# Narrower query chunks and evenly spaced tiles in an attention and FFN kernel

## The chip, the cores and the metric

The program runs on one core of one Trainium2 chip. The metric is the time of one execution on the device in microseconds (us). Before the change it is 531.16 us, the median of 3 runs (530.85 to 532.54). PE is TensorE, PEld its weight loads, DVE VectorE, ACT ScalarE, POOL GpSimd, SP SyncE.

## The reference

One layer over x of 2048 rows and 128 features: an attention with 16 heads of 8 features that has a silu in place of a softmax, then an FFN of width 352 with weights and activations rounded to FP4 in blocks of 16. All values are float32.

```python
x_proj = jax.nn.silu(x @ W1 + b1)
u, v, q, k = jnp.split(x_proj, 4, axis=-1)
scores = jnp.einsum('bqhd,bkhd->bhqk', qh, kh)
attn = jax.nn.silu(scores) / S
av = jnp.einsum('bhqk,bkhd->bqhd', attn, vh).reshape(B, S, D)
y = _layernorm(av * u, gamma, beta) @ W2 + b2
x = _layernorm(x + y)
h = jax.nn.silu(fp4_linear(x, w_gate)) * fp4_linear(x, w_up)
x = _layernorm(x + fp4_linear(h, w_down))
```

## The kernel before

Each of the 16 heads has a silu over 2048 x 2048 scores. The work is cut into chunks of queries (`WIDTHS`), and a chunk of width w into steps: a step takes one tile of 128 keys, and as many heads as fill four banks of 512 columns, twice (`a` = 0, 1). A chunk of 256 queries has 32 steps, two groups of 16 key tiles; one of 128 queries has 16. There are 256 steps, whatever the widths. `BEGIN` holds the first step of each chunk; before, 0, 32, 64, 96, 128, 160, 192, 208, 224, 240.

In a step `at`, PE writes the scores of the step (`scores`, ps<-q_stack,k_stack), in three pairs of PSUM banks that go round (`SB`), then the sums attn x v of the step two earlier (`times_v`, ps<-attn,v_pad; `LAG` = 2), then at most one other job (`job`). ACT applies the silu to each half of the scores (attn<-ps, 128x1024), two a step, and holds three steps of them (`RING`). The scores use bfloat16 parts stacked so that one matmul of 64 rows gives float32 accuracy; the sums are float32 matmuls of 32 columns that the records show in two passes.

The sums of a chunk gather in bank 6 or 7, by turns (`AV`). Meanwhile the other of the two is the spare bank for jobs. When a chunk is done, DVE takes its sums out, times u, into the buffer `zu` (`take_av`, called at the job step LAG after the next chunk's begin). Everything behind the attention is done in 16 tiles of 128 rows. A tile has six jobs on PE, in the spare bank: y (transpose of zu and product with W2), xqT, gate, up, hqT, down. DVE empties the bank after each (two adds or copies, and for y an add only after the row statistics, whose inverse root POOL computes), except gate, which ACT empties with a silu. Between y and xqT, and between up and hqT, DVE does the FP4 rounding in some nine operations; after down it does the last layer norm, and SP writes the tile out. The jobs' steps are a table written by hand (`TILE_AT`: a base step and an offset for each piece); tile 15 comes after all steps.

The engines run their own lists in order and wait on semaphores. Three waits of PE matter. A job waits until the job before it has been emptied, and until `take_av` has been done for the chunk before the one whose sums are being made (`av_taken`). The first sums of a chunk wait until the last job that used their bank has been emptied (`wait_spare`). Scores wait until ACT has read the bank. DVE's list holds the work of each job at the job's step, all of it up to the next job's, so `take_av` stands behind the whole chain of an earlier job.

Of the kernel before, what the change touches and what calls it, by code (L numbers as in the profile page):

```python
# [12 lines left out]
P = 128  # L13
# [9 lines left out]
K_TERMS = (0, 1, 0, 1, 2, 0)  # L23


WIDTHS = (256,) * 6 + (128,) * 4


class Count:
# [10 lines left out]
def build(nc, x, W1, b1, W2, b2, gamma, beta, w_gate, w_up, w_down, out):  # L40
    _, S, D = x.shape
    FF = w_gate.shape[0]
    HD = 8
    CH = 512
    NCH = S // CH
    KT = S // P
    TPC = CH // P
    SLOTS = 8
    M = 4
    FEAT = 3  # L50
    PARTS = 5
    TERMS = len(Q_TERMS)
    RING = 3
    SB = 3
    LAG = 2
# [4 lines left out]
    NBD = D // BLOCK  # L60
    assert D == P and len(FT) == 3 and sum(WIDTHS) == S

# [3 lines left out]

    Q0 = [sum(WIDTHS[:c]) for c in range(len(WIDTHS))]
    STEPS = [(c, g, i) for c, w in enumerate(WIDTHS) for g in range(M * w // CH) for i in range(KT)]
    BEGIN = [STEPS.index((c, 0, 0)) for c in range(len(WIDTHS))] + [len(STEPS)]

    M_ORDER = (0, 2, 1, 3)

    def ms(c, g):

        per = CH // WIDTHS[c]
        return M_ORDER[g * per:(g + 1) * per]

    AV = [6 + c % 2 for c in range(len(WIDTHS))]

# [7 lines left out]
               24: ("q", 1536), 27: ("w2", 0), 29: ("gate", 0), 31: ("up", 0), 33: ("down", 0)}  # L87

    TAIL = KT - 1
    WIDE, DENSE = KT - 6, KT - 2  # L90
    EVEN = {"y": 3, "xqT": 7, "gate": 9, "up": 11, "hqT": 15, "down": 17}
    ODD = {"y": 18, "xqT": 22, "gate": 24, "up": 26, "hqT": 30, "down": 31}
    TILE_AT = {t: (BEGIN[t // 2 + 1], ODD if t % 2 else EVEN) for t in range(WIDE)}
    for t in range(WIDE, DENSE):
        TILE_AT[t] = (BEGIN[WIDE // 2 + 1] + LAG + 12 * (t - WIDE),
                      {"y": 0, "xqT": 4, "gate": 5, "up": 7, "hqT": 10, "down": 11})
    TILE_AT[DENSE] = (BEGIN[-2] + LAG, {"y": 0, "xqT": 4, "gate": 6, "up": 8, "hqT": 12, "down": 13})
    JOB_AT = {at: (kind, i, None) for at, (kind, i) in PREP_AT.items()}
    for t, (base, offsets) in TILE_AT.items():
        JOB_AT |= {base + d: (kind, 0, t) for kind, d in offsets.items()}  # L100
    JOBS = [JOB_AT[at] for at in sorted(JOB_AT)]
    JOB_BANK = [spare_bank(at) for at in sorted(JOB_AT)]
    job_no = {job: k for k, job in enumerate(JOBS)}
    ACT_JOBS = [k for k, (kind, i, tile) in enumerate(JOBS)
                if kind in ("k", "q", "v", "u") or (kind == "gate" and tile is not None)]
    VEC_JOBS = [k for k in range(len(JOBS)) if k not in ACT_JOBS]

    def chunk_of(tile):
        return max(c for c in range(len(WIDTHS)) if Q0[c] <= tile * P)


    UNITS = [("k", 0, 256), ("q", 0, 256), ("k", 256, 512), ("k", 768, 512), ("k", 1280, 512), ("k", 1792, 256),
# [3 lines left out]
    with ExitStack() as ctx:  # L116
        def sb(name, shape, dt=F32):
            return ctx.enter_context(nc.sbuf_tensor(name, shape, dt))

        def sem(name):  # L120
            return ctx.enter_context(nc.semaphore(name))

        ps = ctx.enter_context(nc.psum_tensor("ps", [P, 8, CH], F32))
# [33 lines left out]
        xT = sb("xT", [D, S])  # L157
        feat = sb("feat", [P, FEAT, CH])
        parts = sb("parts", [P, PARTS, 3, CH], BF16)
        uT = sb("uT", [P, S])  # L160
# [4 lines left out]
        k_stack = sb("k_stack", [P, SLOTS, S], BF16)  # L165
        q_stack = sb("q_stack", [P, SLOTS, S], BF16)
        attn = sb("attn", [P, RING, 2, 2, CH])
        zu = sb("zu", [P, CH])

        class Rows:  # L170

# [10 lines left out]
        xqT = sb("xqT", [D, 2, P])  # L182
# [19 lines left out]
        job_made, job_by_act, job_by_vec = sem("job_made"), sem("job_by_act"), sem("job_by_vec")  # L202
# [31 lines left out]
        def stack(eng, n, chosen=range(TERMS), by_pool=False):  # L234
# [3 lines left out]
            for part in range(3):  # L238
                eng.wait_ge(split_done, 3 * n + part + 1)
                for t in (t for t in chosen if terms[t] == part):  # L240
                    eng.dma_start(to[t::8, :, start:start + w], parts[:, n % PARTS, part, 0:w]).then_inc(done, 16)

# [3 lines left out]
        def wait_stack(eng, n):  # L246
            if n < len(SHARES):
                eng.wait_ge(stacked[n], 16 * len(SHARES[n][0]))
                eng.wait_ge(stacked_by_pool[n], 16 * len(SHARES[n][1]))
            else:  # L250
                eng.wait_ge(stacked[n], 16 * TERMS)
# [128 lines left out]
        def _(pe):  # L380
            def mm(to, lhsT, rhs, start=True, stop=True):
                return pe.matmul(to, lhsT, rhs, start=start, stop=stop, skip_group_check=True)  # L382
# [139 lines left out]

            def y_of(tile, small, off):

                c = chunk_of(tile)
                z = zu[:, tile * P - Q0[c]:(tile + 1) * P - Q0[c]]
                pe.transpose(ps[:, small, off:off + P], z, ident[:, :])  # L527
                return mm(ps[:, small, off + P:off + 2 * P], z, w2_centred[:, :])

# [11 lines left out]
            def behind(kind, tile, bank):  # L541
                r = ROWS[tile % 2]
                if kind == "y":
                    return y_of(tile, bank, 0)
                if kind == "xqT":
                    pe.wait_ge(xq_ready, tile + 1)
                    return pe.transpose(ps[:, bank, 0:P], r.xn[:, 0:D], ident[:, :])
                if kind == "gate":
                    return mm(ps[:, bank, 0:FF], xqT[:, tile % 2, :], wgate_t[:, :])
                if kind == "up":  # L550
                    return mm(ps[:, bank, 0:FF], xqT[:, tile % 2, :], wup_t[:, :])
                if kind == "hqT":
                    pe.wait_ge(hq_ready, tile + 1)
                    return hqT_of(r, bank)
                return down_of(r, bank, 0)
# [16 lines left out]
            for i in range(KT - TAIL):  # L572
                y_of(TAIL + i, TAIL_SMALL[i], 0).then_inc(tail_y, 1)
# [20 lines left out]
        def _(act):  # L594
            def silu(to, frm, **kw):
                return act.activation(to, frm, ACT.Silu, **kw)  # L596
# [5 lines left out]
            def project(kind, c, bank):  # L602
# [7 lines left out]
                w = UNITS[n][2]  # L610
                if n >= FEAT:
                    act.wait_ge(split_done, 3 * (n - FEAT + 1))
                return silu(feat[:, n % FEAT, 0:w], ps[:, bank, 0:w],
                            bias=b1_col[:, 1:2] if kind == "q" else b1_col[:, 2:3])
# [60 lines left out]
        def _(dve):  # L675
# [16 lines left out]
            def split(kind, start):  # L692
# [4 lines left out]
                else:  # L697
                    dve.wait_ge(job_by_act, ACT_JOBS.index(job_no[(kind, start, None)]) + 1)
                if n >= PARTS:
                    wait_stack(dve, n - PARTS)  # L700
                f, p = feat[:, n % FEAT, 0:w], parts[:, n % PARTS, :, 0:w]
                dve.tensor_copy(p[:, 0, :], f).then_inc(split_done, 1)  # L702
# [51 lines left out]
            def take_av(c):  # L754

                w = WIDTHS[c]
                dve.wait_ge(av_done, BEGIN[c + 1])
                for tile in range(TAIL):
                    if chunk_of(tile) == c - 1:
                        dve.wait_ge(job_made, job_no[("y", 0, tile)] + 1)  # L760
                dve.scalar_tensor_tensor(out=zu[:, 0:w], in0=ps[:, AV[c], 0:w], scalar=1.0 / S,
                                         in1=uT[:, Q0[c]:Q0[c] + w], op0=ALU.mult, op1=ALU.mult).then_inc(av_taken, 1)

            def statistics(src, which, r):
# [129 lines left out]
            for at in range(BEGIN[1], len(STEPS)):  # L894
                if at - LAG in BEGIN:
                    take_av(BEGIN.index(at - LAG) - 1)
                kind, _, tile = JOB_AT.get(at, (None, None, None))
                if tile is None:
                    continue
                if kind == "y":  # L900
                    to_quantised_x(tile)
                elif kind == "xqT":
                    copy_xqT(tile)
                elif kind == "up":
                    to_quantised_h(tile)
                elif kind == "hqT":
                    copy_hqT(tile)
                elif kind == "down":
                    to_out(tile)

            take_av(len(WIDTHS) - 1)
            for i, r in enumerate(TAIL_ROWS):
                dve.wait_ge(tail_y, i + 1)
# [38 lines left out]
```

## Time and profile before

| | |
|---|---|
| median of 3 runs | 531.16 us |
| the profiled execution | 531.98 us, span 530.0 us |
| busy PE, ACT, DVE, POOL | 96%, 93%, 40%, 12% of the span |
| first and last step's activations | 16.84 us to 507.2 us |
| granted TensorE clock | 0.997 of full speed in the mean, 9 tenths or more in every slice but one |
| DMA busy | almost all before 80 us |

The page gives one execution. Busy time of PE is modelled from pipelined matmuls, so a busy PE may still be waiting; the views in order of time tell more. A line is often that of a helper (`mm`, `silu`), so groups are read by the names of what they write and read. ACT's activations overlap: one starts about 0.9 us after the one before, and lasts 1.02 us or more.

### The profile page before, as it was taken

The numbers are of one execution on the slowest core, as the hardware profiler recorded it, in microseconds if no ns is written. First come the engines' busy times: TensorE is split into PE (matmuls) and PEld (weight loads), VectorE is DVE, ScalarE is ACT, GpSimd is POOL, SyncE is SP. The second block draws the span as 40 slices with busy tenths as digits, with TensorE's granted clock in tenths as the row PEclk, the third lists the DMA queues.
The fourth block names the chain that finished last, engine by engine and source line by source line (L and its number), as shares of the span: only waits on it lengthen the run. The fifth ranks groups of instructions, "written<-read, shape, count | busy, mean of one in ns | idle before, by whom it ended". The sixth has DMA issues, their size and how long they took to land.

```text
span 530.0 us, 18169 instructions
## 1 busy us (share of the span) xinstructions
PE 510.5 (96%) x8116; PEld 268.8 (51%) x8116; DVE 210.2 (40%) x621; ACT 493.1 (93%) x558; POOL 63.4 (12%) x152
## 2 busy tenths in 40 slices
PE   7799999999999999999999999999999999999996
PEld 5354444444444444444444444444477777777753
DVE  4644642243433332333333332333343444544344
ACT  4799999999999999999999999999999999999920
POOL 6940000101010100101010100101010110101010
PEclk9899999999999999999999999999999999999999
DMA  4891240000000000000000000000000000000000
GB/s 125 219 189 29 66 119 2 2 2 7 1 7 2 6 2 8 1 2 6 2 8 1 7 1 7 1 2 8 1 9 2 9 9 3 9 4 7 4 6 7
DMA packets 13576, 12.00 MB, mean 23 GB/s; under 512 B 1589, under 2 KB 12858, under 8 KB 13498
## 3 DMA queue, kind: packets, MB, share of 16 engines
q1 hardware_dynamic: 12650, 9.05, 6.9%
q0 software_dynamic: 704, 1.66, 1.3%
q8 instruction: 64, 1.05, 0.8%
q10 hardware_dynamic: 144, 0.13, 0.1%
q14 instruction: 14, 0.11, 0.1%
HBM read 1.92 MB, written 1.05 MB: 6 GB/s over the span
## 4 chain that ended last, share of the span: by engine, by line
ACT 45%; PE 39%; issue 10%; DVE 3%; DMA 1%; POOL 1%; SPq 0%; POOLq 0%; DVEq 0%; ACTq 0%
ACT attn L596 44%; PE ps L382 36%; PE ps L532 1%; DMA k_stack<-parts 1%; PE ps L414 1%; POOL rstd_b L370 1%; PE ps L527 0%; DMA xn_b<-in_L_attn_b 0%; DVE parts L702 0%; DVE stats_b L765 0%; ACT gate_a L596 0%; POOL ve_b L369 0%; DVE mv_b L767 0%; DVE x_b L770 0%; ACT feat L596 0%
## 5 line engine op out<-in xcount | busy, mean ns | idle before, releaser
L596 ACT ACTIVATE attn<-ps 128x1024 f32<-128x1024 f32 x512 | 477.5, 1125 | 7.2 <-PE ps L382 5.7
L382 PE MATMUL ps<-attn,v_pad 128*32 128x256 f32 (+1 forms) x5120 | 275.4, 342 | 0.4 <-DVE wdown_t L890 0.3
L382 PE MATMUL ps<-q_stack,k_stack 64*128 64x256 bf16 (+1 forms) x2560 | 170.3, 251 | 8.2 <-DMA q_stack<-parts 1.4
L382 PEld LDWEIGHTS ps<-attn,v_pad 128*32 128x32 f32 x5120 | 132.5, 109 | 80.8 <-issue 37.9
L382 PEld LDWEIGHTS ps<-q_stack,k_stack 64*128 64x128 bf16 x2560 | 81.2, 94 | 119.6 <-ACT attn L596 75.8
L369 POOL TENSOR_TENSOR ve_a<-mv_a,eps_col 128x1 f32<-128x1 f32 x24 | 4.5, 189 | 270.1 <-DVE mv_a L767 270.1
L815 DVE TENSOR_TENSOR gate_a<-gate_a,ps 128x352 f32<-128x352 f32 x8 | 4.2, 521 | 58.7 <-PE ps L382 58.7
L369 POOL TENSOR_TENSOR ve_b<-mv_b,eps_col 128x1 f32<-128x1 f32 x24 | 4.6, 190 | 177.2 <-DVE mv_b L767 177.2
L815 DVE TENSOR_TENSOR gate_b<-gate_b,ps 128x352 f32<-128x352 f32 x7 | 3.6, 521 | 50.6 <-PE ps L382 50.6
L382 PE MATMUL ps<-zeros 128*128 128x512 bf16 x63 | 15.7, 399 | 1.2 <-DVE zeros L836 1.2
L702 DVE CAST parts<-feat 128x512 bf16<-128x512 f32 (+1 forms) x10 | 6.1, 611 | 25.6 <-ACT feat L596 25.6
L382 PE MATMUL ps<-wgate_t,xqT 128*128 128x352 f32 x32 | 13.7, 511 | 0.0
L382 PE MATMUL ps<-wup_t,xqT 128*128 128x352 f32 x32 | 13.6, 508 | 0.0
L370 POOL TENSOR_TENSOR rstd_a<-ve_a,minus_half 128x1 f32<-128x1 f32 x24 | 13.2, 550 | 1.9
L370 POOL TENSOR_TENSOR rstd_b<-ve_b,minus_half 128x1 f32<-128x1 f32 x24 | 13.2, 548 | 1.9
L770 DVE TENSOR_SCALAR x_b<-x1p_b,mv_b,rstd_b 128x128 f32<-128x128 f32 x16 | 5.5, 347 | 14.9 <-POOL rstd_b L370 14.9
L770 DVE TENSOR_SCALAR x_a<-x1p_a,mv_a,rstd_a 128x128 f32<-128x128 f32 x16 | 5.5, 347 | 14.9 <-POOL rstd_a L370 14.9
L829 DVE TENSOR_TENSOR x1p_a<-ps,x_a 128x128 f32<-128x128 f32 x8 | 2.3, 292 | 22.6 <-PE ps L382 22.6
L382 PE MATMUL ps<-xT,w_qk 128*128 128x512 f32 (+1 forms) x20 | 10.3, 612 | 0.5 <-ACT xT L627 0.5
L382 PEld LDWEIGHTS ps<-zeros 128*128 128x128 bf16 x63 | 6.2, 101 | 8.2 <-issue 1.2
L823 DVE COPY hqT_a<-ps 128x256 f32<-128x256 f32 x8 | 3.4, 425 | 16.7 <-PE ps L532 16.7
L765 DVE BATCH_NORM_STATS2 stats_a<-ps 128x6 f32<-128x128 f32 x8 | 2.4, 298 | 19.0 <-PE ps L382 19.0
(153 smaller groups left out, 345.0 us busy)
## 6 DMA issues: line engine op xcount, KB each, us to landing
k_stack<-parts SPq DMA_DIRECT2D x18, 128.0 KB, 5.2
q_stack<-parts SPq DMA_DIRECT2D x18, 128.0 KB, 2.4
q_stack<-uT SPq DMA_DIRECT2D x2, 448.0 KB, 8.1
x_sb<-in_L_attn_x SPq DMA_DIRECT2D x3, 256.0 KB, 4.3
k_stack<-parts SPq DMA_DIRECT2D x10, 64.0 KB, 3.9
k_stack<-uT POOLq DMA_DIRECT2D x2, 320.0 KB, 5.2
q_stack<-parts SPq DMA_DIRECT2D x8, 64.0 KB, 2.0
out<-x_a SPq DMA_DIRECT2D x8, 64.0 KB, 1.5
```

Source lines behind the costliest of these rows:

```text
L369: link(pool.tensor_tensor(r.ve[:, :], r.mv[:, which, 1:2], eps_col[:, :], ALU.add))
L370: pool.tensor_tensor(r.rstd[:, which:which + 1], r.ve[:, :], minus_half[:, :], ALU.pow).then_inc(rstd_ready, 1)
L382: return pe.matmul(to, lhsT, rhs, start=start, stop=stop, skip_group_check=True)
L414: last = pe.transpose(ps[:, bank, i * P:(i + 1) * P], x_sb[:, start // P + i, :], ident[:, :])
L532: last = pe.transpose(ps[0:fn, bank, t * P:(t + 1) * P], r.xn[:, f0:f0 + fn], ident[:, :])
L596: return act.activation(to, frm, ACT.Silu, **kw)
L702: dve.tensor_copy(p[:, 0, :], f).then_inc(split_done, 1)
L765: dve.bn_stats(r.stats[:, :], src)
L770: return dve.tensor_scalar(to, src, r.mv[:, which, 0:1], r.rstd[:, which:which + 1], ALU.subtract, ALU.mult)
L815: dve.tensor_tensor(r.gate[:, :], r.gate[:, :], ps[:, bank, 0:FF], ALU.mult).then_inc(job_by_vec, 1)
L823: dve.tensor_copy(r.hqT[:, 0:2, :].rearrange("p t n -> p (t n)"), ps[:, bank, 0:2 * P])
L829: dve.tensor_tensor(r.x1p[:, :], ps[:, bank, 0:D], r.x1[:, :], ALU.add).then_inc(job_by_vec, 1)
```

## The change

`WIDTHS` becomes one chunk of 256 and fourteen of 128, so `BEGIN` is 0, 32, 48, 64, and so on by 16 to 240. The tiles 0 to 14 get one table of offsets, that of tile 14 before, and bases spread evenly from step 35 to 242: 35, 49, 64, 79, 94, 108, 123, 138, 153, 168, 182, 197, 212, 227, 242. Before, the tiles 0 to 9 lay in pairs on the wide chunks, with 2 steps between hqT and down in the even ones and 1 in the odd ones, 10 to 13 followed each other every 12 steps, and 14 was where it is now. `zu` becomes a ring of four slots of 128 rows; a chunk's sums wait only for the y of the tile four before. The number of matmuls of scores and sums in a 128-wide step is twice that of a 256-wide one, each half as wide.

```diff
--- before.py
+++ after.py
@@ -23,7 +23,7 @@
 K_TERMS = (0, 1, 0, 1, 2, 0)
 
 
-WIDTHS = (256,) * 6 + (128,) * 4
+WIDTHS = (256,) + (128,) * 14
 
 
 class Count:
@@ -48,6 +48,7 @@
     SLOTS = 8
     M = 4
     FEAT = 3
+    ZU = 4
     PARTS = 5
     TERMS = len(Q_TERMS)
     RING = 3
@@ -87,14 +88,10 @@
                24: ("q", 1536), 27: ("w2", 0), 29: ("gate", 0), 31: ("up", 0), 33: ("down", 0)}
 
     TAIL = KT - 1
-    WIDE, DENSE = KT - 6, KT - 2
-    EVEN = {"y": 3, "xqT": 7, "gate": 9, "up": 11, "hqT": 15, "down": 17}
-    ODD = {"y": 18, "xqT": 22, "gate": 24, "up": 26, "hqT": 30, "down": 31}
-    TILE_AT = {t: (BEGIN[t // 2 + 1], ODD if t % 2 else EVEN) for t in range(WIDE)}
-    for t in range(WIDE, DENSE):
-        TILE_AT[t] = (BEGIN[WIDE // 2 + 1] + LAG + 12 * (t - WIDE),
-                      {"y": 0, "xqT": 4, "gate": 5, "up": 7, "hqT": 10, "down": 11})
-    TILE_AT[DENSE] = (BEGIN[-2] + LAG, {"y": 0, "xqT": 4, "gate": 6, "up": 8, "hqT": 12, "down": 13})
+    FIRST_AT = BEGIN[1] + LAG + 1
+    SPAN = BEGIN[-2] + LAG - FIRST_AT
+    TILE_AT = {t: (FIRST_AT + SPAN * t // (TAIL - 1), {"y": 0, "xqT": 4, "gate": 6, "up": 8, "hqT": 12, "down": 13})
+               for t in range(TAIL)}
     JOB_AT = {at: (kind, i, None) for at, (kind, i) in PREP_AT.items()}
     for t, (base, offsets) in TILE_AT.items():
         JOB_AT |= {base + d: (kind, 0, t) for kind, d in offsets.items()}
@@ -104,9 +101,6 @@
     ACT_JOBS = [k for k, (kind, i, tile) in enumerate(JOBS)
                 if kind in ("k", "q", "v", "u") or (kind == "gate" and tile is not None)]
     VEC_JOBS = [k for k in range(len(JOBS)) if k not in ACT_JOBS]
-
-    def chunk_of(tile):
-        return max(c for c in range(len(WIDTHS)) if Q0[c] <= tile * P)
 
 
     UNITS = [("k", 0, 256), ("q", 0, 256), ("k", 256, 512), ("k", 768, 512), ("k", 1280, 512), ("k", 1792, 256),
@@ -165,7 +159,7 @@
         k_stack = sb("k_stack", [P, SLOTS, S], BF16)
         q_stack = sb("q_stack", [P, SLOTS, S], BF16)
         attn = sb("attn", [P, RING, 2, 2, CH])
-        zu = sb("zu", [P, CH])
+        zu = sb("zu", [P, ZU * P])
 
         class Rows:
 
@@ -522,8 +516,7 @@
 
             def y_of(tile, small, off):
 
-                c = chunk_of(tile)
-                z = zu[:, tile * P - Q0[c]:(tile + 1) * P - Q0[c]]
+                z = zu[:, tile % ZU * P:(tile % ZU + 1) * P]
                 pe.transpose(ps[:, small, off:off + P], z, ident[:, :])
                 return mm(ps[:, small, off + P:off + 2 * P], z, w2_centred[:, :])
 
@@ -755,10 +748,10 @@
 
                 w = WIDTHS[c]
                 dve.wait_ge(av_done, BEGIN[c + 1])
-                for tile in range(TAIL):
-                    if chunk_of(tile) == c - 1:
-                        dve.wait_ge(job_made, job_no[("y", 0, tile)] + 1)
-                dve.scalar_tensor_tensor(out=zu[:, 0:w], in0=ps[:, AV[c], 0:w], scalar=1.0 / S,
+                tile = Q0[c] // P
+                if tile >= ZU:
+                    dve.wait_ge(job_made, job_no[("y", 0, tile - ZU)] + 1)
+                dve.scalar_tensor_tensor(out=zu[:, tile % ZU * P:tile % ZU * P + w], in0=ps[:, AV[c], 0:w], scalar=1.0 / S,
                                          in1=uT[:, Q0[c]:Q0[c] + w], op0=ALU.mult, op1=ALU.mult).then_inc(av_taken, 1)
 
             def statistics(src, which, r):
```

What moves on PE shows at three places. First, PE around the y of tile 1, before. There the job stands at step 50, in a chunk that began at 32 (ps<-q_stack,k_stack are the scores, ps<-attn,v_pad the sums):

```order
362 L382 MATMUL ps<-attn,v_pad 32x256 [waits attn_ready]
363 L382 MATMUL ps<-attn,v_pad 32x256 x7
364 L527 MATMUL ps<-ident,zu 128x128 [waits av_taken,job_by_vec]
365 L382 MATMUL ps<-w_centred,zu 128x128
366 L382 MATMUL ps<-q_stack,k_stack 128x256 [waits attn_ready]
367 L382 MATMUL ps<-q_stack,k_stack 128x256 x3
368 L382 MATMUL ps<-q_stack,k_stack 128x256 [waits attn_ready]
369 L382 MATMUL ps<-q_stack,k_stack 128x256 x3
370 L382 MATMUL ps<-attn,v_pad 32x256 [waits attn_ready]
371 L382 MATMUL ps<-attn,v_pad 32x256 x7
```

and after, where the job stands at step 49, one step past the begin of the chunk at 48:

```order
356 L376 MATMUL ps<-attn,v_pad 32x128 [waits attn_ready]
357 L376 MATMUL ps<-attn,v_pad 32x128 x15
358 L520 MATMUL ps<-ident,zu 128x128 [waits av_taken,job_by_vec]
359 L376 MATMUL ps<-w_centred,zu 128x128
360 L376 MATMUL ps<-q_stack,k_stack 128x128 [waits attn_ready]
361 L376 MATMUL ps<-q_stack,k_stack 128x128 x7
362 L376 MATMUL ps<-q_stack,k_stack 128x128 [waits attn_ready]
363 L376 MATMUL ps<-q_stack,k_stack 128x128 x7
364 L376 MATMUL ps<-attn,v_pad 32x128 [waits job_by_vec,attn_ready]
365 L376 MATMUL ps<-attn,v_pad 32x128 x15
```

The same job now comes before the first sums of a new chunk, and these wait for it (job_by_vec) as well as for ACT (attn_ready).

Second, PE at steps 129 and 130, before:

```order
886 L382 MATMUL ps<-attn,v_pad 32x256 [waits attn_ready]
887 L382 MATMUL ps<-attn,v_pad 32x256 x7
888 L382 MATMUL ps<-q_stack,k_stack 128x256 [waits attn_ready]
889 L382 MATMUL ps<-q_stack,k_stack 128x256 x3
890 L382 MATMUL ps<-q_stack,k_stack 128x256 [waits attn_ready]
891 L382 MATMUL ps<-q_stack,k_stack 128x256 x3
892 L382 MATMUL ps<-attn,v_pad 32x256 [waits job_by_vec,attn_ready]
893 L382 MATMUL ps<-attn,v_pad 32x256 x7
```

and after:

```order
889 L376 MATMUL ps<-attn,v_pad 32x128 [waits attn_ready]
890 L376 MATMUL ps<-attn,v_pad 32x128 x15
891 L376 MATMUL ps<-wgate_t,xqT 128x352 [waits av_taken,job_by_vec]
892 L376 MATMUL ps<-q_stack,k_stack 128x128 [waits attn_ready]
893 L376 MATMUL ps<-q_stack,k_stack 128x128 x7
894 L376 MATMUL ps<-q_stack,k_stack 128x128 [waits attn_ready]
895 L376 MATMUL ps<-q_stack,k_stack 128x128 x7
896 L376 MATMUL ps<-attn,v_pad 32x128 [waits job_by_act,attn_ready]
897 L376 MATMUL ps<-attn,v_pad 32x128 x15
```

The first sums of the chunk at 128 waited for a job that DVE empties, placed three steps before. Now they wait for the gate of tile 6 (job_by_act), placed one step before.

Third, PE from the down piece of tile 13 (ps<-wdown_t,hqT_b) to the y of tile 14 (ps<-ident,zu), before:

```order
1638 L382 MATMUL ps<-wdown_t,hqT_b 128x128 [waits av_taken,job_by_vec]
1639 L382 MATMUL ps<-wdown_t,hqT_b 128x128 x2
1640 L382 MATMUL ps<-q_stack,k_stack 128x128 [waits attn_ready]
1641 L382 MATMUL ps<-q_stack,k_stack 128x128 x7
1642 L382 MATMUL ps<-q_stack,k_stack 128x128 [waits attn_ready]
1643 L382 MATMUL ps<-q_stack,k_stack 128x128 x7
1644 L382 MATMUL ps<-attn,v_pad 32x128 [waits job_by_vec,attn_ready]
1645 L382 MATMUL ps<-attn,v_pad 32x128 x15
1646 L527 MATMUL ps<-ident,zu 128x128 [waits av_taken,job_by_vec]
1647 L382 MATMUL ps<-w_centred,zu 128x128
```

and after:

```order
1636 L376 MATMUL ps<-q_stack,k_stack 128x128 [waits attn_ready]
1637 L376 MATMUL ps<-q_stack,k_stack 128x128 x7
1638 L376 MATMUL ps<-attn,v_pad 32x128 [waits attn_ready]
1639 L376 MATMUL ps<-attn,v_pad 32x128 x15
1640 L376 MATMUL ps<-q_stack,k_stack 128x128 [waits attn_ready]
1641 L376 MATMUL ps<-q_stack,k_stack 128x128 x7
1642 L376 MATMUL ps<-q_stack,k_stack 128x128 [waits attn_ready]
1643 L376 MATMUL ps<-q_stack,k_stack 128x128 x7
1644 L376 MATMUL ps<-attn,v_pad 32x128 [waits job_by_vec,attn_ready]
1645 L376 MATMUL ps<-attn,v_pad 32x128 x15
1646 L520 MATMUL ps<-ident,zu 128x128 [waits av_taken,job_by_vec]
1647 L376 MATMUL ps<-w_centred,zu 128x128
```

After the change the down piece stands earlier (rows 1632 and 1633, ahead of these), so one more step of scores and sums lies between it and that y.

## Rows read from the trace of the kernel before

**Rows 1.** The page, part 1: busy time, share, instructions of each engine.

```profile
PE 510.5 (96%) x8116; PEld 268.8 (51%) x8116; DVE 210.2 (40%) x621; ACT 493.1 (93%) x558; POOL 63.4 (12%) x152
```

**Rows 2.** ACT in order of time, two windows: start, busy us, line, operation, count.

```profile
145.38 17.52 ACT L596 ACTIVATE attn<-ps 128x1024 f32<-128x1024 f32 x19
...
145.38 19.36 ACT L596 ACTIVATE attn<-ps 128x1024 f32<-128x1024 f32 x21
...
164.94 27.88 ACT L596 ACTIVATE attn<-ps 128x1024 f32<-128x1024 f32 x30
...
193.02 14.13 ACT L596 ACTIVATE attn<-ps 128x1024 f32<-128x1024 f32 x15
```

**Rows 3.** PE in order of time: two starts of scores at either width.

```profile
168.66 0.61 PE L382 MATMUL ps<-q_stack,k_stack 64*128 64x256 bf16 x8
...
170.21 0.84 PE L382 MATMUL ps<-q_stack,k_stack 64*128 64x256 bf16 x8
...
402.84 0.62 PE L382 MATMUL ps<-q_stack,k_stack 64*128 64x128 bf16 x16
...
404.40 0.62 PE L382 MATMUL ps<-q_stack,k_stack 64*128 64x128 bf16 x16
```

**Rows 4.** ACT in order of time, around one tile's gate.

```profile
444.21 2.04 ACT L596 ACTIVATE attn<-ps 128x1024 f32<-128x1024 f32 x2
446.13 0.48 ACT L596 ACTIVATE gate_a<-ps 128x352 f32<-128x352 f32 x1
446.48 1.05 ACT L596 ACTIVATE attn<-ps 128x1024 f32<-128x1024 f32 x1
```

**Rows 5.** ACT in order of time, first and last group of steps 192 to 255.

```profile
384.71 15.69 ACT L596 ACTIVATE attn<-ps 128x1024 f32<-128x1024 f32 x17
...
495.18 12.05 ACT L596 ACTIVATE attn<-ps 128x1024 f32<-128x1024 f32 x13
```

**Rows 6.** ACT in order of time, with idle time before, at two tiles' ends.

```profile
457.03 6.74 ACT L596 ACTIVATE attn<-ps 128x1024 f32<-128x1024 f32 x7 [0.33 <-PE ps L382]
...
474.90 4.80 ACT L596 ACTIVATE attn<-ps 128x1024 f32<-128x1024 f32 x5
...
479.87 1.94 ACT L596 ACTIVATE attn<-ps 128x1024 f32<-128x1024 f32 x2 [0.17 <-PE ps L382]
...
482.93 3.77 ACT L596 ACTIVATE attn<-ps 128x1024 f32<-128x1024 f32 x4 [1.12 <-PE ps L382]
```

**Rows 7.** All engines in order of time, a tile's piece y and its emptying.

```profile
458.15 0.33 PE L527 MATMUL ps<-ident,zu 128*128 128x128 f32 x1
...
458.63 0.62 PE L382 MATMUL ps<-q_stack,k_stack 64*128 64x128 bf16 x16
...
459.18 1.08 PE L382 MATMUL ps<-attn,v_pad 128*32 128x128 f32 x32
...
460.24 0.35 DVE L775 SCALAR_TENSOR_TENSOR x1p_b<-ps,rstd_b,x_sb 128x128 f32<-128x128 f32 x1 [0.93 <-POOL rstd_b L370]
```

**Rows 8.** All engines in order of time: down piece, taking of sums, next y.

```profile
478.57 0.94 PE L382 MATMUL ps<-wdown_t,hqT_b 128*128 128x128 f32 x6
...
481.61 0.28 DVE L761 SCALAR_TENSOR_TENSOR zu<-ps,uT 128x128 f32<-128x128 f32 x1
...
482.04 0.30 PE L527 MATMUL ps<-ident,zu 128*128 128x128 f32 x1 [0.97 <-DVE zu L761]
```

**Rows 9.** PE in order of time: scores, up piece, scores.

```profile
446.34 0.62 PE L382 MATMUL ps<-q_stack,k_stack 64*128 64x128 bf16 x16
...
447.90 0.86 PE L382 MATMUL ps<-wup_t,xqT 128*128 128x352 f32 x2
...
448.69 0.62 PE L382 MATMUL ps<-q_stack,k_stack 64*128 64x128 bf16 x16
```

**Rows 10.** All engines in order of time: copy of hqT, and sums beside it.

```profile
504.96 0.28 DVE L824 COPY hqT_a<-ps 96x128 f32<-96x128 f32 x1
...
505.07 1.08 PE L382 MATMUL ps<-attn,v_pad 128*32 128x128 f32 x32
```

## The prediction

> **What bounds the kernel now.** I read the busy times first, and the reader is to see two engines that look full: PE at 96% and ACT at 93% [rows 1]. The second view, ACT in order of time, tells them apart. In an undisturbed stretch of a 256-wide chunk 19 activations of 128x1024 take 17.52 us [rows 2]; the first takes 1.02 us, as any does after a stall (1.94 us for two: 1.02 + 0.92 [rows 6]), so each further one ends 0.917 us after the one before. That is ACT's own pace, and I count losses against it by ends: the starts come slightly closer and the durations grow, so a late start of up to some 0.2 us can cost nothing. A step (two activations) is 1.83 us. The third view, PE in order of time, shows what a step costs PE when it waits for nothing: 168.66 to 170.21 at width 256, 402.84 to 404.40 at width 128, so 1.55 and 1.56 us [rows 3]. ACT is the bound, PE gains 0.27 us a step on it, and PE's lead is limited by its three pairs of score banks. So the kernel loses time where PE runs out of lead: at the jobs of the tiles, and at waits of PE for DVE or ACT.
>
> Price of the losses before. Wide chunk: from 145.38 to 207.15 (193.02 + 14.13) there are 66 activations and two gate activations [rows 2]. A gate activation costs 0.36 (ends 446.25 and 447.53, less 0.92 [rows 4]). 61.77 - 1.02 - 65 x 0.917 - 2 x 0.36 = 0.43; with 0.9167 unrounded 0.45. There are five such chunks with two tiles each: 2.3 us. The dense part, 384.71 to 507.23 (495.18 + 12.05), has 64 steps, so 128 activations, and five gates [rows 5]: 122.52 - 1.02 - 127 x 0.9167 - 5 x 0.36 = 3.3 us. Together 5.6 us between steps 32 and 255. Of the dense part's loss 1.12 + 0.11 = 1.23 us is one event, before the activation at 482.93 [rows 6] (0.11 is added to an idle time shown, since the first activation after it takes 1.02 instead of 0.917).
>
> **The change part by part.**
>
> Width. Ten more groups of 16 steps run with 128-wide matmuls: 16 + 32 instead of 8 + 16 records of PE a step, and as many weight loads more. By [rows 3] that costs PE 0.01 us a step, hidden under ACT's 1.83. The bounds for it are 0 and, if no weight load overlapped anything, far more (rivals). I take 0. DVE gets ten 128-wide takings of the sums for five 256-wide ones, each about 0.28 us [rows 8], on an engine that is 40% busy [rows 1].
>
> A rule of the Trainium skill speaks against this. "TensorE: Matmul & The Clock Gate", section Back-to-back issue gap, puts a stream of weight load and matmul pairs at about 81 ns a pair for 128 columns. By it a step of 48 pairs would take 3.9 us (an estimate from that page), over twice ACT's 1.83. The trace disagrees: 48 pairs pass in 1.56 us, 33 ns each, in the steps that are 128 wide already [rows 3]; the measurement decides.
>
> Tiles. There are 14 tiles to place before the last overlapped one, whose pieces stay where they are. Each now has its hqT piece and its down piece on neighbouring steps (hqT +12, down +13). Of that pair before: ACT had ended 474.90 + 4.80 = 479.70, and its next activation ended 479.87 + 1.02 = 480.89, so 1.19 - 0.92 = 0.27 to 0.28 us are lost [rows 6]. 14 x 0.265 (one step more passes since the gate piece, so a little more of the late start is absorbed) = 3.7 us. The piece y takes PE 458.15 to 458.63 = 0.48 us [rows 7]. Directly after down, PE has no lead: the seven activations from 457.03 take 6.74 - 1.02 - 6 x 0.917 = 0.22 us too long [rows 6]. With one free step between, PE has 0.27 back, and 1.56 + 0.48 - 1.83 = 0.21 is covered: nothing. The new spacing gives the neighbour three times (tiles 1, 5, 10): 3 x 0.22 = 0.65 us. Gate and up cost nothing by themselves, as in the wide chunks. The base of the new placement is 3.7 + 0.65 = 4.3 us, against 5.6. In it the 1.23 us are gone: there y waited for DVE to finish the down piece of the tile before and then take the sums, which ended 481.89, 3.3 us after the start of that piece at 478.57 [rows 8]. Now a free step lies between (third place in the order), y's turn comes 0.87 + 2 x 1.56 = 4.0 us after that start, and the taking is done.
>
> New waits at chunk boundaries. Two steps after a chunk begins, its first sums (a matmul ps<-attn,v_pad, in PE's order behind the scores) wait for the job that last used their bank. There are twice as many boundaries early on, and the jobs drift across them. I went through all: three have a job one step after the boundary's begin whose emptying is slow.
>
> (a) Step 50, tile 1's y at step 49 (first place in the order). DVE empties y's bank only after statistics and a round over POOL: y started 458.15, the emptying add ended 460.24 + 0.35 = 460.59 [rows 7], 2.44 later. PE resumes 0.15 behind DVE (481.89 to 482.04 [rows 8]), so the sums start 2.59 after y instead of 1.03 (459.18 [rows 7]): 1.56 late. Queued behind them on PE are the next scores, for which ACT waits; PE has 0.27 of lead. Loss 1.29 us.
>
> (b) Step 130, tile 6's gate at step 129 (second place). The emptying is ACT's gate activation, which stands behind an activation of step 130. In the like frame it ended 446.13 + 0.48 = 446.61 [rows 4]; sums would start about 446.7 and the next scores 1.0 later (1.56 less the 0.55 between scores and sums, 458.63 to 459.18 [rows 7]) at 447.7, instead of 446.34 [rows 9]: 1.37 late. Lead is 0.27 + 0.36 (ACT's own time for the gate) = 0.63, loss 0.74. And the up piece follows in the next step without that lead: it takes PE 447.90 to 448.69 = 0.79 [rows 9], 1.56 + 0.79 - 1.83 = 0.52. Together 1.26 us.
>
> (c) Step 210, tile 11's hqT at step 209: the sums start 505.07 in the like frame, the copy ends 504.96 + 0.28 and 0.15 to resume gives 505.39 [rows 10]: 0.32 late, all lost, as the down piece follows.
>
> The other boundaries end in nothing: up at +1 (tile 8) waits for one DVE operation that PE's scores cover; gate or down at +0 is emptied a step earlier; y at +0 (tile 2) is emptied just in time (2.59 against 0.48 + 1.56 + 0.55 = 2.59), bounds 0 to 0.3, I take 0. For tiles 1 to 4 the taking of sums now stands on DVE between y's chain and the xqT copy: 0.15 to 0.28 us later for xqT, which the lead regained until the gate covers; bounds 0 to 0.25 a tile, I take 0. Output DMAs move with their tiles; no engine waits for one but two tiles later.
>
> Sum after: 3.7 + 0.65 + 1.29 + 1.26 + 0.32 = 7.2 us, before 5.6: 1.6 to 1.7 us slower. The profiled execution took 531.98 us with a span of 530.0; it becomes 533.6. It stands 0.8 over the median of 531.16, which becomes 532.8. The part before step 32 and the tail after the last activation keep their order.
>
> **The rivals.** Within 0.3% (1.6 us) a measurement of this kernel can't tell a change from none; the forecast lies on that line.
>
> *The bank waits are covered.* One mechanism with one place: (a) to (c) cost nothing since PE holds more lead there than I give it, or the emptying is earlier. Then 4.3 against 5.6 remains: 529.9, not slower. For it: no row of before has sums that wait for y or a gate, so 2.59 and 1.37 are put together from pieces. Against it: each piece is a row, and nothing in PE's order between them can shift. It decides for faster once the three cost under 1.3 us together in place of 2.9.
>
> *Spacing of two steps is not enough.* y two steps after down loses its 0.22 each of 11 times, since the regained 0.27 is only 0.06 above the need: 2.4 us more, 535.2. For it: the margin is thin. Against it: PE's steady 1.56 [rows 3].
>
> *Weight loads bound PE.* If scores and sums did not overlap their loads, a step of width 128 would take over ACT's 1.83; at only 0.1 us over it, 160 more such steps give 16 us: 549. Against it: free steps of width 128 ran at 1.56 [rows 3]. One in a hundred. The rule of the Trainium skill quoted above ("TensorE: Matmul & The Clock Gate", Back-to-back issue gap) is this mechanism.
>
> *The change doesn't do what it says*, PE's order at the boundaries being other than I read it: the order of instructions shows the waits, so I give it nothing.
>
> **How the numbers follow.** Forecast 0.70 (531.8 to 533.9), bank waits covered 0.14, spacing too small 0.12, weight loads 0.01, the rest for something unseen, 0.03. Of the forecast a little over half lies above 532.75. Slower 0.39 + 0.12 + 0.01 = 0.52, same 0.31 + 0.10 = 0.41, faster 0.04 + 0.03 = 0.07 (529.9 is itself 0.24% below, so only part of that rival counts as faster). The range takes in the forecast's bounds and part of the covered case, and ends short of the spacing case: 530.2 to 534.9; left out are most of the spacing case and the lower part of the covered one.
>
> **What would show it.** Right: ACT idle for PE by over 1 us at the step after chunk begin 48, some 0.7 us with a further slip at 130, none before tile 14's y; PE at 1.56 us in free 128-wide steps; clock 1.00 throughout. Wrong: idle for PE shortly after every y, or a free step of PE over 1.83 us, or DVE's taking of the sums as the releaser of PE's jobs.

## The result, and the profile after

The changed kernel takes 533.88 us (median of 18 runs, 532.58 to 534.83) beside 532.20 for the kernel before (18 runs, 530.85 to 533.33): the ratio is 1.0027, 95% interval 1.0015 to 1.0039. It is slower (the interval lies above 1), by an amount on the line of 0.3%. The forecast was 532.8 us with 531.16 before, so +1.64 us and a ratio of 1.0031.

The profiled execution took 534.20 us with a span of 532.1, 2.1 more than before. I split it in three. Up to the first activation of step 32 it is 85.90 us beside 85.46; this part, in which the loads arrive, lay between 84.3 and 88.1 in the nine profiles of this study and follows no kernel. The part behind the last activation is 22.79 us in both. Between, from the end of the first activation of step 32 (85.90 + 1.11 = 87.01) to the end of the last (509.35), it is 422.34 us, where it was 420.65 (86.58 to 507.23): +1.69 us. That part ("the steps" below) is free of the noise of the loads. Each figure of it comes from one profiled execution, but where the kernels have the same jobs it repeats: from the first activation of step 214 to the last it is 77.68 us by the ends in the changed kernel, e1, e2, e4 and e5 alike. So the experiments are read there, and the timed ratios stand beside it.

In the first part PE waits for the DMA of `q_stack`: 0.6 and 0.7 us in the profiles at 84.4 and 84.3 (e4_y2, e5_no_waits), 1.2 to 2.8 in the others. The granted TensorE clock goes with it: over the first 50 us it is 1.00 of full speed in those two and 0.90 to 0.97 in the others, where it is at the lower of its two levels (1.2 GHz) for a stretch that starts after PE began to wait. That the wait brings the clock down is not shown. From 50 us to the last activation it is 1.00 in all nine.

The changed kernel's page answers [rows 1] with half again as many records on PE. Its weight loads are busy 68% instead of 51% of the span, and the other engines are as before:

```profile
PE 511.6 (96%) x11956; PEld 360.6 (68%) x11956; DVE 211.1 (40%) x626; ACT 493.0 (93%) x558; POOL 63.3 (12%) x152
```

ACT of the changed kernel in order of time, from tile 0's gate to tile 2's (start, busy us, idle before in brackets):

```profile
105.56 12.05 ACT L589 ACTIVATE attn<-ps 128x1024 f32<-128x1024 f32 x13
117.77 3.99 ACT L589 ACTIVATE attn<-ps 128x1024 f32<-128x1024 f32 x4 [0.16 <-PE ps L376]
122.94 10.19 ACT L589 ACTIVATE attn<-ps 128x1024 f32<-128x1024 f32 x11 [1.18 <-PE ps L376]
133.00 0.48 ACT L589 ACTIVATE gate_b<-ps 128x352 f32<-128x352 f32 x1
133.35 12.05 ACT L589 ACTIVATE attn<-ps 128x1024 f32<-128x1024 f32 x13
145.56 15.69 ACT L589 ACTIVATE attn<-ps 128x1024 f32<-128x1024 f32 x17 [0.16 <-PE ps L376]
```

Each tile ends with 0.16 us of idle at down, so 0.16 + 0.11 = 0.27 lost. Behind it the 17 activations from 145.56 take 15.69 = 1.02 + 16 x 0.917: tile 2's y, two steps after down, costs nothing. The four from 117.77, with tile 1's y directly behind down, take 3.99 - 1.02 - 3 x 0.917 = 0.22 too long. Then comes the first new wait, 1.18 + 0.11 = 1.29 us. All engines there, which answers [rows 7]:

```profile
118.89 0.33 PE L520 MATMUL ps<-ident,zu 128*128 128x128 f32 x1
...
119.38 0.62 PE L376 MATMUL ps<-q_stack,k_stack 64*128 64x128 bf16 x16
...
120.98 0.35 DVE L768 SCALAR_TENSOR_TENSOR x1p_b<-ps,rstd_b,x_sb 128x128 f32<-128x128 f32 x1 [0.93 <-POOL rstd_b L364]
...
121.48 1.08 PE L376 MATMUL ps<-attn,v_pad 128*32 128x128 f32 x32 [1.48 <-DVE x1p_b L768]
...
122.50 0.62 PE L376 MATMUL ps<-q_stack,k_stack 64*128 64x128 bf16 x16
```

The sums start 2.59 us after y, released by DVE's add, as forecast. The second new wait, at tile 6's gate, answers [rows 4, 9]:

```profile
269.83 0.86 PE L376 MATMUL ps<-wgate_t,xqT 128*128 128x352 f32 x2
...
270.63 0.62 PE L376 MATMUL ps<-q_stack,k_stack 64*128 64x128 bf16 x16
271.99 0.48 ACT L589 ACTIVATE gate_a<-ps 128x352 f32<-128x352 f32 x1
...
272.61 1.08 PE L376 MATMUL ps<-attn,v_pad 128*32 128x128 f32 x32 [1.36 <-ACT gate_a L589]
...
274.06 1.94 ACT L589 ACTIVATE attn<-ps 128x1024 f32<-128x1024 f32 x2 [0.68 <-PE ps L376]
...
275.18 0.86 PE L376 MATMUL ps<-wup_t,xqT 128*128 128x352 f32 x2
...
276.41 9.27 ACT L589 ACTIVATE attn<-ps 128x1024 f32<-128x1024 f32 x10 [0.41 <-PE ps L376]
```

PE waits for the gate activation, ACT then idles 0.68 and, since up follows without lead, 0.41 more: 0.79 + 0.52 = 1.31 us. The third shows as an idle time of 0.48 in place of 0.16:

```profile
425.15 5.61 ACT L589 ACTIVATE attn<-ps 128x1024 f32<-128x1024 f32 x6 [0.48 <-PE ps L376]
```

At tile 14, where 1.12 us of idle stood before [rows 6], PE now comes to y at 484.07, when DVE has long taken the sums (483.12 + 0.28), and ACT runs 17 activations without a loss:

```profile
481.39 15.69 ACT L589 ACTIVATE attn<-ps 128x1024 f32<-128x1024 f32 x17 [0.16 <-PE ps L376]
...
483.12 0.28 DVE L754 SCALAR_TENSOR_TENSOR zu<-ps,uT 128x128 f32<-128x128 f32 x1
...
484.07 0.33 PE L520 MATMUL ps<-ident,zu 128*128 128x128 f32 x1
```

### The profile page after: what moved, and what is told of

Read it like the earlier page. It is cut to its first block, busy times and chain, and to the rows that moved or that the text cites. A ratio compares the mean times of both kernels' runs of the same rounds, so it can differ in the third digit from the quotient of the medians.

```text
span 532.1 us, 25862 instructions
## 1 busy us (share of the span) xinstructions
PE 511.6 (96%) x11956; PEld 360.6 (68%) x11956; DVE 211.1 (40%) x626; ACT 493.0 (93%) x558; POOL 63.3 (12%) x152
## 4 chain that ended last, share of the span: by engine, by line
ACT 51%; PE 33%; issue 12%; DVE 2%; POOL 1%; DMA 1%; SPq 0%; POOLq 0%; DVEq 0%; ACTq 0%
ACT attn L589 49%; PE ps L376 31%; PE ps L525 1%; PE ps L520 1%; DMA q_stack<-parts 1%; DMA xn_b<-in_L_attn_b 0%; ACT feat L589 0%; ACT gate_a L589 0%; POOL rstd_b L364 0%; ACT gate_b L589 0%; POOL q_stack L235 0%; POOL k_stack L235 0%; DVE magic_b L838 0%; ACT v_sb L589 0%; DVE stats_b L758 0%
## 5 line engine op out<-in xcount | busy, mean ns | idle before, releaser
L376 PE MATMUL ps<-attn,v_pad 128*32 128x128 f32 (+1 forms) x7680 | 276.2, 283 | 3.5 <-DVE x1p_b L768 1.5
L376 PEld LDWEIGHTS ps<-attn,v_pad 128*32 128x32 f32 x7680 | 195.6, 109 | 39.0 <-issue 6.7
L376 PE MATMUL ps<-q_stack,k_stack 64*128 64x128 bf16 (+1 forms) x3840 | 170.1, 222 | 7.6 <-DMA q_stack<-parts 2.6
L376 PEld LDWEIGHTS ps<-q_stack,k_stack 64*128 64x128 bf16 x3840 | 109.9, 94 | 86.0 <-ACT attn L589 47.9
L695 DVE CAST parts<-feat 128x512 bf16<-128x512 f32 (+1 forms) x10 | 3.7, 373 | 30.8 <-ACT feat L589 30.8
L816 DVE COPY hqT_b<-ps 128x256 f32<-128x256 f32 x7 | 3.0, 425 | 17.4 <-PE ps L525 17.4
```

The costliest lines, as they stand in the source:

```text
L816: dve.tensor_copy(r.hqT[:, 0:2, :].rearrange("p t n -> p (t n)"), ps[:, bank, 0:2 * P])
```

## The experiments

All are edits of the changed kernel, whose steps take 422.34 us. By the timed ratios alone e1_tile1, e2_gate6 and e6_gap2 can't be told from the kernel before, nor e4_y2 from the changed one; what they show is in the steps.

| kernel | steps, us | against the changed kernel | time against before, 95% interval |
|---|---|---|---|
| before | 420.65 | -1.69 | 1 |
| changed | 422.34 | 0 | 1.0027 (1.0015 to 1.0039) |
| e1_tile1 | 421.05 | -1.29 | 1.0003 (0.9989 to 1.0017) |
| e2_gate6 | 421.02 | -1.32 | 1.0008 (0.9996 to 1.0020) |
| e3_widths | 426.12 | +3.77 | 1.0107 (1.0088 to 1.0126) |
| e4_y2 | 423.49 | +1.15 | 1.0036 (1.0017 to 1.0054) |
| e5_no_waits | 419.64 | -2.71 | 0.9979 (0.9966 to 0.9992) |
| e6_gap2 | 419.66 | -2.68 | 0.9988 (0.9971 to 1.0005) |
| e7_both | 416.84 | -5.51 | 0.9936 (0.9919 to 0.9954) |

**Tile 1's y off the boundary (e1_tile1).**

```diff
+    TILE_AT[1] = (50, TILE_AT[1][1])
```

> The changed kernel with tile 1 one step later (base 50 in place of 49), so that its y no longer stands one step past the begin of the chunk at 48. Theory (sums wait for the bank that y used): the loss of ACT after step 50 of the changed kernel, 1.29 us (ends later than 0.917 us a piece), goes. The 0.22 us of y directly behind down moves from tile 1 to tile 2 (down at 63, y at 64). Span from step 32 to 255 shorter by 1.29 us. Rival (the loss belongs to y behind down and DVE being behind, wherever it stands): the loss moves with the neighbours to tile 2's y, and the time stays.

Measured -1.29 us. The idle time of 1.18 is gone, and the 0.22 of y behind down has moved to tile 2. DVE is there as far behind as it was at tile 1 (its last operation for the tile before starts 0.35 us after y, 147.30 to 147.65; it was 118.89 to 119.25), and nothing beyond the 0.22 is lost. The wait for the bank is the cause, and the rival falls.

**Tile 6's gate one step earlier (e2_gate6).**

```diff
+    TILE_AT[6] = (TILE_AT[6][0], TILE_AT[6][1] | {"gate": 5})
```

> The changed kernel with the gate of tile 6 one step earlier (step 128 in place of 129), all else the same. Theory (sums at step 130 wait for ACT's gate activation): the 0.79 us after step 130 and the 0.52 us of up after step 131 both go, since up then has its lead again; gate costs at most 0.1 us more right behind xqT. Steps 32 to 255 shorter by 1.2 to 1.3 us. Rival (the loss comes from the gate and up pieces being short of lead, not from the bank): gate one step earlier leaves 0.5 us or more at up.

Measured -1.32 us, both parts. ACT of this kernel runs through gate and up of tile 6 with no idle time:

```profile
267.37 3.00 ACT L590 ACTIVATE attn<-ps 128x1024 f32<-128x1024 f32 x3
270.25 0.48 ACT L590 ACTIVATE gate_a<-ps 128x352 f32<-128x352 f32 x1
270.59 10.22 ACT L590 ACTIVATE attn<-ps 128x1024 f32<-128x1024 f32 x11
```

**The widths alone, tiles where they stood before (e3_widths).**

```diff
-    TILE_AT = {t: (FIRST_AT + SPAN * t // (TAIL - 1), ...)
...
+    TILE_AT = {t: (32 * (t // 2 + 1), ODD if t % 2 else EVEN) for t in range(10)}
+    for t in range(10, 14):
+        TILE_AT[t] = (194 + 12 * (t - 10), {"y": 0, "xqT": 4, "gate": 5, "up": 7, "hqT": 10, "down": 11})
...
```

> The new widths and the ring of four alone: the tiles' jobs stand at the steps they had before the change. Theory: width itself costs nothing (a free step of PE 1.56 us, ACT 0.917 a piece). But the five odd tiles of the first ten now have y at the step where the sums of a chunk are first taken, directly behind down, so that each waits for DVE to finish down's chain and take the sums, as tile 14's did before: 1.23 us in place of 0.2 each, five times. Steps 32 to 255: 5.2 us longer than before the change, 3.5 longer than after it, about 537.4 beside 532.2. Rival (width costs something in each step): losses of like size spread over free steps too, and over 1 us more than that. Rival (only the width mattered and the steps are free): the time of before.

Measured +3.77 against the changed kernel, +5.47 against before. Each of the five odd tiles loses 1.23 us at y, as tile 14 did before. All engines at the second of them, tile 3, from down to ACT's next activation:

```profile
179.03 0.94 PE L378 MATMUL ps<-wdown_t,hqT_a 128*128 128x128 f32 x6
...
181.81 0.34 DVE L765 TENSOR_SCALAR x_a<-x1p_a,mv_a,rstd_a 128x128 f32<-128x128 f32 x1 [0.93 <-POOL rstd_a L366]
182.08 0.28 DVE L756 SCALAR_TENSOR_TENSOR zu<-ps,uT 128x128 f32<-128x128 f32 x1
182.51 0.30 PE L522 MATMUL ps<-ident,zu 128*128 128x128 f32 x1 [0.97 <-DVE zu L756]
...
183.40 1.02 ACT L591 ACTIVATE attn<-ps 128x1024 f32<-128x1024 f32 x1 [1.12 <-PE ps L378]
```

Free steps lose nothing. What the width does cost shows only where PE has no lead: the down pieces of the first ten tiles lose 0.024 (even) and 0.04 us (odd) more than at width 256, 0.3 us over the ten. That is the part of +5.47 that the expectation (+5.2) left out. Both rivals fall.

**A y one step past a boundary, with lead (e4_y2).**

```diff
+    TILE_AT[2] = (65, TILE_AT[2][1])
```

> The changed kernel with tile 2 one step later (base 65 in place of 64), so that its y stands one step past the begin of the chunk at 64, but three steps behind down in place of one. Theory with lead: y's bank is emptied 2.59 us after y starts whatever the lead, but PE starts y earlier against ACT, so less is lost than the 1.29 of tile 1: about 1.0 us, plus 0.22 for tile 3's y now directly behind down. Together 1.2 us longer than the changed kernel. Rival (a bank wait costs its 1.29 whatever the lead): 1.5 us longer. Rival (no bank wait, y at tile 1 cost for another reason): 0.2 us longer.

Measured +1.15: 0.94 at the new wait and 0.21 at tile 3's y. PE and DVE there:

```profile
148.34 0.33 PE L521 MATMUL ps<-ident,zu 128*128 128x128 f32 x1
...
150.42 0.35 DVE L769 SCALAR_TENSOR_TENSOR x1p_a<-ps,rstd_a,x_sb 128x128 f32<-128x128 f32 x1 [0.93 <-POOL rstd_a L365]
...
150.92 1.08 PE L377 MATMUL ps<-attn,v_pad 128*32 128x128 f32 x32 [1.47 <-DVE x1p_a L769]
...
152.37 1.02 ACT L590 ACTIVATE attn<-ps 128x1024 f32<-128x1024 f32 x1 [0.83 <-PE ps L377]
```

The sums again start 2.58 us after y, and ACT loses 0.94 instead of 1.29. So the wait is as long with more lead, and the loss is what the lead does not cover; the rivals at 1.5 and 0.2 us fall.

**All three waits away (e5_no_waits).**

```diff
+    TILE_AT[1] = (50, TILE_AT[1][1])
+    TILE_AT[6] = (TILE_AT[6][0], TILE_AT[6][1] | {"gate": 5})
+    TILE_AT[11] = (198, TILE_AT[11][1])
```

> The changed kernel without its three bank waits: tile 1 at base 50, gate of tile 6 one step earlier, tile 11 at base 198 in place of 197 (its hqT then stands two steps past the chunk's begin; tile 12's y comes directly behind down for it). Theory: 1.29 + 1.31 + 0.32 us go, 0.22 for tile 12's y comes: steps 32 to 255 shorter by 2.7 us than in the changed kernel and 1.0 shorter than before the change, about 531.3 beside 532.4. Rival (the two larger ones share lead and do not add up): under 2.3 us.

Measured -2.71: the three add up. The kernel is now faster than before the change, 0.9979. Without the three waits the new placement is worth 1.0 us of steps against before; the waits turned that into +1.69.

**A free step before down (e6_gap2).**

```diff
-    ... {"y": 0, "xqT": 4, "gate": 6, "up": 8, "hqT": 12, "down": 13})
+    ... {"y": 0, "xqT": 4, "gate": 6, "up": 8, "hqT": 11, "down": 13})
```

> The changed kernel with hqT one step earlier in every tile (offset 11 in place of 12), so that a free step lies between hqT and down; the three bank waits stay (the third moves to tile 10). Theory: PE regains 0.27 us between the two pieces, and the loss at down falls from 0.265 to 0.06 us (0.058 in the even tiles of the kernel with widths alone); 14 times 0.2 is 2.9 us, and the third wait shrinks as well: 3.1 us shorter than the changed kernel. Rival (three steps are too few for DVE's rounding between up and hqT, and PE waits there instead): under 1.5 us shorter.

Measured -2.68, most of it as expected: ten tiles lose 0.06 us at down. The rest of the expectation fails at four: tiles 8 and 9 lose 0.165 each, tile 6 0.14, and tile 10, which has the third wait now, 0.33. At 8 and 9 DVE's taking of the sums stands between up and hqT in its list. DVE and PE at tile 8's hqT (ps<-ident,xn_a):

```profile
335.59 0.52 DVE L740 TENSOR_TENSOR xn_a<-xn_a,scale_a 128x352 f32<-128x352 f32 x1
336.04 0.28 DVE L754 SCALAR_TENSOR_TENSOR zu<-ps,uT 128x128 f32<-128x128 f32 x1
336.42 0.52 PE L525 MATMUL ps<-ident,xn_a 128*128 128x128 f32 x3
```

PE starts 0.10 us behind the end of the taking (336.32), and 0.11 later than the sums before it would let it (they start at 335.30 and take 1.01). At tile 6 it starts 0.15 us behind the end of the rounding itself (280.34 to 280.49). So three steps are just too few in these places, and the rival is right there, for 0.1 us each, but not in its size (under 1.5 us shorter).

**Both (e7_both).**

```diff
...
+    AT = (35, 50, 64, 79, 94, 109, 124, 138, 153, 168, 183, 197, 212, 227, 242)
+    TILE_AT = {t: (AT[t], {"y": 0, "xqT": 4, "gate": 6, "up": 8, "hqT": 11, "down": 13}) for t in range(TAIL)}
```

> Both: hqT at offset 11 with a free step before down, and bases 35, 50, 64, 79, 94, 109, 124, 138, 153, 168, 183, 197, 212, 227, 242, with which no y, gate or hqT stands one step past a chunk's begin. Theory: left are 14 times 0.06 and three times 0.2 (the y pieces at 64, 138 and 197 directly behind down): 1.4 us of loss in place of 7.2, so 5.8 us shorter than the changed kernel and 4.1 shorter than before the change, 528.3 beside 532.4 (ratio 0.992). Rival (ACT has a further floor that shows once PE is never late): more than 1 us of loss in free steps.

Measured -5.51 us against the changed kernel, -3.81 against before, and 0.9936 (0.9919 to 0.9954) in time: 528.77 us, the fastest of all. ACT of this kernel never idles for 0.15 us or more between steps 32 and 255. Two stretches from gate to gate look like this:

```profile
189.87 27.69 ACT L587 ACTIVATE attn<-ps 128x1024 f32<-128x1024 f32 x30
217.44 0.48 ACT L587 ACTIVATE gate_a<-ps 128x352 f32<-128x352 f32 x1
217.78 27.69 ACT L587 ACTIVATE attn<-ps 128x1024 f32<-128x1024 f32 x30
```

The 0.3 us missing are in the tiles 8, 9 and 10, which lose 0.165 each at down where the others lose 0.06. In all three the taking of the sums stands between up and hqT, as in e6. This cause is read from the traces; no run moved the taking alone. No further floor of ACT appears.

## Why the prediction was right

*Width costs nothing.* Right for free steps (1.56 us, 122.50 to 124.06 in the changed kernel), and e3_widths shows no loss in them. At down it costs 0.02 to 0.04 us a tile, which the forecast had in without naming it, since it took down's 0.27 from 128-wide steps [rows 6]. In the changed kernel too the 48 pairs of such a step pass in 1.56 us, 33 ns each. The rule of 81 ns a pair, from the Trainium skill's page "TensorE: Matmul & The Clock Gate" (Back-to-back issue gap), does not hold for these matmuls, whose weights are 64x128 and 128x32.

*The base, 4.3 us.* Fourteen downs at 0.264 to 0.268 and three y pieces at 0.215 make 4.36. Spacing of two steps was enough: y lost nothing in any of eleven places, so that rival falls. The 1.23 us of tile 14 are gone, as worked out.

*The new waits, 2.9 us.* Measured 1.29, 1.31 and 0.32 for 1.29, 1.26 and 0.32. Only the second was 0.05 low: PE resumed 0.14 us behind the gate's end, where the forecast had allowed 0.09 (446.61 to 446.7). e1 and e2 take the first two away one by one, e4 makes one like them, and e5 takes all three away, so their causes are shown, not only argued. The third has no run of its own; in e5 ACT's idle time at that down falls from 0.48 us to the 0.16 of the other tiles. No other boundary lost anything.

*The size.* +1.69 us in the steps for a forecast of 1.6 to 1.7. What was worse founded was the starting point: the median of three runs was 531.16, and of 18 it is 532.20, so the absolute 532.8 was 1.1 us low while the difference was right. The times go with the mean granted clock of the execution. Beside e1_tile1 the kernel before took 531.17 us (median of 6) where that was 0.998 or more, and 532.64 (median of 19) where it was less; the changed kernel took 532.84 (8) and 534.27 (10), some 1.65 more in either case. Two of the first three executions, 531.16 and 530.85, are as short as the former, so the median of three lay low by the luck of the draw. The profiles put this spread into the first 32 steps, with PE's wait for a load and the lower clock.

*Chances.* The forecast said slower by over 0.3% with 0.52 and within 0.3% with 0.41. The ratio 1.0027 has its interval on both sides of 1.003, so the runs can't tell these two; that it is slower than before they do tell.

## What to carry to other kernels

Find the engine that sets the pace, count its losses by the ends of its instructions, and give each piece of side work the lead that the feeding engine has at its place. The wait behind y was as long at two different leads (2.59 and 2.58 us from y to the sums); what it cost depended on the lead. A free step between two pieces made y free (0.22 us without it) and down nearly so (0.06 in place of 0.27). When side work is spread evenly over a structure with another period, some piece lands on each bad place: one table entry moved by one step was worth 1.3 us here, beside 1.7 for the whole change, so choose the places and leave the spacing a little uneven.

## What the runs showed of the hardware

ACT's back-to-back activations of 128x1024 start 0.904 us apart and end 0.917 us apart, the recorded duration growing by 13 ns each from 1.02 us, up to 1.42 us (before step 32). A late start takes the growth back before it costs anything: before tile 14's gate in the kernel before, a start 0.12 us late lost nothing in the ends. Counting starts against 0.904 us would have put the losses before the change at some 11 us instead of 5.6.

PE, waiting for DVE's semaphore, resumed 0.15 us after the end of the DVE operation (121.33 to 121.48), and waiting for ACT's 0.14 us after (272.47 to 272.61).
